# Decoder layer on one core: FFN stages one tile nearer to the attention, z and hidden scales computed apart, the last norms in two steps of the tail

## What is computed

```python
x = x + attn(layernorm(x))      # q * scan(kv, sigmoid(a)): a gated recurrence over the sequence
x = x + xattn(layernorm(x))     # 16 heads over 64 context rows and a null row, Wout, layernorm, scale and bias
x = x + ffn(layernorm(x))

def act_quant(x):               # per row
    scale = 127.0 / clip(max(abs(x), axis=-1), 1e-5)
    return clip(round(x * scale), -128, 127) / scale
def ffn(x):                     # weights are ternary, 256 -> 1024 -> 256
    h = silu(bitlinear(x, w_gate)) * bitlinear(x, w_up)
    return bitlinear(h, w_down) # bitlinear quantises its input with act_quant
```

## Time and profile before

| | |
|---|---|
| median of 3 runs | 542.71 us (541.34 to 543.03) |
| the profiled execution | 541.14 us, of which the span 539.1 us |
| TensorE busy | 483.1 us (90%) |
| VectorE busy | 425.2 us (79%) |
| ScalarE busy | 327.6 us (61%) |
| GpSimd busy | 304.4 us (56%) |

### The profile page before, as it was taken

How to read it: one execution, slowest core, us unless ns; L and a number is a source line. 1 busy time by engine, 2 the same in 40 slices (tenths; PEclk the granted TensorE clock), 3 DMA queues, 4 the chain that set the end, 5 groups by cost and what they waited for, 6 DMA issues and landing times.

```text
span 539.1 us, 9354 instructions
## 1 busy us (share of the span) xinstructions
PE 483.1 (90%) x2974; PEld 390.8 (72%) x3002; DVE 425.2 (79%) x937; ACT 327.6 (61%) x452; POOL 304.4 (56%) x482
## 2 busy tenths in 40 slices
PE   1889999999988988999999999999999999997662
PEld 1666787777767888877877887878778878776321
DVE  5899998958527666888888888888888888875863
ACT  4422233356333443797888877878888778866450
POOL 2211323710001567778787877787878777888631
PEclk9999999999999999999999999999999999999995
DMA  8992000000000000011322121212111322122342
GB/s 284 364 400 85 1 0 1 0 2 1 1 0 1 1 2 5 7 30 35 47 44 49 36 55 35 50 36 55 40 45 36 47 47 45 36 54 50 69 97 68
DMA packets 57949, 30.49 MB, mean 57 GB/s; under 512 B 44336, under 2 KB 55856, under 8 KB 57904
## 3 DMA queue, kind: packets, MB, share of 16 engines
q1 hardware_dynamic: 57904, 29.93, 21.5%
HBM read 15.24 MB, written 4.19 MB: 36 GB/s over the span
## 4 chain that ended last, share of the span: by engine, by line
POOL 32%; issue 23%; PE 20%; DVE 18%; DMA 4%; ACT 2%; POOLq 1%; DVEq 1%; ACTq 0%
PE psum L1130 9%; POOL region_d L529 5%; POOL region_d L507 3%; POOL xs L509 3%; POOL region_d L505 3%; PE psum L1146 3%; POOL sc L539 3%; POOL sc L552 3%; DVE region_a L871 3%; POOL region_d L563 2%; POOL region_d L520 2%; POOL region_c L568 2%; PE psum L1387 2%; DMA region_d<-region_d 2%; PE psum L1392 2%
## 5 line engine op out<-in xcount | busy, mean ns | idle before, releaser
L517 POOL TENSOR_TENSOR region_d<-region_d,rden 128x1024 f32<-128x1024 f32 x32 | 60.9, 1902 | 103.4 <-DVE rden L998 103.4
L1130 PE MATMUL psum<-Mhi,xT2hi 128*128 128x260 f32 x256 | 75.0, 293 | 0.2
L1130 PE MATMUL psum<-Mhi,xT2lo 128*128 128x260 f32 x256 | 72.4, 283 | 0.0
L1130 PE MATMUL psum<-Mlo,xT2hi 128*128 128x260 f32 x256 | 72.4, 283 | 0.0
L1387 PE MATMUL psum<-VW,region_d 128*128 128x256 f32 x256 | 61.1, 381 | 4.6 <-DVE pTn L1047 4.6
L1392 PE MATMUL psum<-VW,region_d 128*128 128x256 f32 x256 | 60.5, 379 | 0.0
L1011 DVE SCALAR_TENSOR_TENSOR region_c<-psum,zw,region_c 128x1024 f32<-128x1024 f32 x29 | 37.2, 1283 | 28.7 <-ACT region_c L689 28.6
L1387 PEld LDWEIGHTS psum<-VW,region_d 128*128 128x128 f32 x256 | 48.1, 190 | 14.6 <-DVE pTn L1047 6.0
L1392 PEld LDWEIGHTS psum<-VW,region_d 128*128 128x128 f32 x256 | 48.6, 190 | 6.6
L677 ACT ACTIVATE region_d<-psum,sc 128x256 f32<-128x256 f32 x32 | 18.0, 564 | 53.9 <-POOL sc L556 53.1
L981 DVE TENSOR_REDUCE mx<-psum 128x8 f32<-128x520 f32 x64 | 44.2, 691 | 6.6 <-PE psum L1130 5.3
(11 more groups left out here) (150 smaller groups left out, 1253.5 us busy)
## 6 DMA issues: line engine op xcount, KB each, us to landing
out_dram<-xs SPq DMA_DIRECT2D x32, 128.0 KB, 1.9
xs<-in_x_dram SPq DMA_DIRECT2D x1, 2560.0 KB, 16.5
VW<-in_L_xattn_Wkv_dram SPq DMA_DIRECT2D x1, 2048.0 KB, 17.3
region_b<-in_L_xattn_Wkv_dram SPq DMA_DIRECT2D x1, 2048.0 KB, 17.6
xs<-in_x_dram SPq DMA_DIRECT2D x3, 512.0 KB, 6.5
region_w<-in_L_ffn_w_gate_dram SPq DMA_DIRECT2D x1, 1024.0 KB, 10.1
region_w<-in_L_ffn_w_up_dram SPq DMA_DIRECT2D x1, 1024.0 KB, 12.5
region_w<-in_L_ffn_w_down_dram SPq DMA_DIRECT2D x1, 1024.0 KB, 16.6
```

What stands on the lines that cost most here:

```text
L517: pool.tensor_tensor(p2[:, v, 0:H * MK].rearrange("p (h j) -> p h j", j=MK), e[:, :, 0:MK], rden[:, v, :].unsqueeze(2).broadcast_to([P, H, ...
L1130: mm = pe.matmul(dst, lhsT, rhs, start=i == 0, stop=i == len(terms) - 1)
```

## The change

The FFN stages of a tile move one step nearer to its attention: gate, up, silu and hidden row are those of tile n - 4 in step n, quantisation, cast and transpose of the hidden row those of n - 5, down, residual and store those of n - 6. The loop has one step less (to T + 5). `norm3` stays with tile n - 3, but stands on ScalarE right behind `norm_out` in all steps; the maximum and scale of z stand on VectorE ahead of `exp_sum`; the quantisation of z stands on GpSimd between the output and the probabilities. The scale of the hidden row has instructions of its own in all steps. The waits for `consts_set` that stood beside other waits in this loop are gone. In the tail, the norms of the tiles 29 to 31 are done in the steps 32 and 33.

```diff
-            for n in range(-2, T + 7):
+            for n in range(-2, T + 6):
...
             def stages2_3(n, u4):
-                u, v = u4 % 2, 1 - u4 % 2
+                if n == T:
+                    deviation4(T - 2)
+                    quantise_z(T - 3)
+                if n == T + 1:
+                    quantise_z(T - 1)
                 if exists(n - 1, T):
...
+                    add_output(n - 1)
+                if not late(n) and exists(n - 3, T):
+                    quantise_z(n - 3)
                 if exists(n + 1, T):
...
+                    probabilities(n + 1)
+                if exists(n - 5, T):
+                    cast_h(n - 5)
+                if n == T:
+                    deviation4(T - 1)
+                    quantise_z(T - 2)
+                if not late(n) and exists(n - 2, T):
+                    deviation4(n - 2)
                 if exists(n, T):
...
+                    deviation3(n)
             steps(stages2_3)
...
-                    count, = registers(pool, n + 1)
-                    pool.wait_ge(consts_set, 2)
-                    pool.wait_ge(rstd3_done, count)
...
-                if late(n) and exists(n - 3, T):
-                    norm3(n, v)
+                if n <= T and exists(n - 3, T):
+                    norm3(n - 3)
+                if n == T + 1:
+                    norm3(T - 1)
                 if exists(n, T):
...
+                if late(n) and exists(n - 4, T):
+                    silu_gate(n - 4, False)
+                if exists(n - 5, T):
+                    quantise_h(n - 5, n)
+                if n == T:
+                    norm3(T - 2)
+                if not late(n) and exists(n - 4, T):
+                    silu_gate(n - 4, n < T - 1)
                 if even:
...
+            def scale_hidden(t, v):
+
+                dve.wait_ge(hmax_done, t + 1)
+                dve.tensor_scalar(qs[:, v, 0:1], amax[:, v, 0:1], CLIP, 1.0 / QMAX, ALU.max, ALU.mult) \
+                    .then_inc(qsh_done, 1)
+                dve.wait_ge(qsh_done, t + 1)
+                dve.reciprocal(qr[:, v, 0:1], qs[:, v, 0:1]).then_inc(qrh_done, 1)
+                hidden_weight(t, v)
...
+                if exists(n - 3, T) and n <= T:
+                    z_max(n - 3)
+                    scale_z(n - 3)
                 if not head and exists(n + 1, T):
                     exp_sum(n + 1, v)
...
+                if not late(n) and exists(n - 4, T):
+                    hidden_layer(n - 4, n)
+                if n == T + 1:
+                    z_max(T - 1)
+                    scale_z(T - 1)
...
                 if late(n):
-                    residual(n - 7)
...
+                    residual(n - 6)
+                    if exists(n - 4, T):
+                        hidden_layer(n - 4, n)
+                if exists(n - 4, T):
+                    hidden_max(n - 4, v)
+                    scale_hidden(n - 4, v)
+                if n == T:
+                    stats4(T - 1)
+                    mean4(T - 1)
+                    z_max(T - 2)
+                    scale_z(T - 2)
+                if not late(n) and exists(n - 6, T):
+                    residual(n - 6)
```

More of the change, by code:

```diff
@@ L377, in late, with hidden @@
             return isinstance(n, int) and n >= T
-        def hidden(n):
-            return h3[1 if isinstance(n, int) and n >= T - 5 and (n - (T - 5)) % 2 == 0 else 0]
+        def hidden(t):
+            return h3[1 if t >= T - 4 and (t - (T - 4)) % 2 == 0 else 0]
         def half(n):
@@ new lines, in cast_h, with deviation4 @@
+            def cast_h(t):
+                pool.wait_ge(hq_done, t + 1)
+                if t > 0:
+                    pool.wait_ge(nhT_ready[(t - 1) % 2], 16 * ((t - 1) // 2 + 1))
+                pool.tensor_copy(nh3, nq3).then_inc(nh_ready, 1)
+            def deviation4(t):
+                u = t % 2
+                pool.wait_ge(mv4_done, t + 1)
+                if t > 1:
+                    pool.wait_ge(z_ready, t - 1)
+                pool.tensor_scalar(sc4[:, u, 0:1], mv4[:, u, 1:2], 1e-5, None, ALU.add).then_inc(ve4_done, 1)
+                pool.wait_ge(ve4_done, t + 1)
+                pool.tensor_tensor(sc4[:, u, 1:2], sc4[:, u, 0:1], expo[:, 0:1], ALU.pow).then_inc(rstd4_done, 1)
+                pool.wait_ge(rstd4_done, t + 1)
+                pool.tensor_scalar(sc4[:, u, 2:3], mv4[:, u, 0:1], sc4[:, u, 1:2], -1.0, ALU.mult, ALU.mult) \
+                    .then_inc(nmr4_done, 1)
@@ new lines, in quantise_z @@
+            def quantise_z(t):
+                v = t % 2
+                pool.wait_ge(qr_done, t + 1)
+                pool.tensor_scalar(z3[:, v, :], z3[:, v, :], qr[:, v, 1:2], MAGIC, ALU.mult, ALU.add) \
+                    .then_inc(zq_done, 1)
+                pool.wait_ge(zq_done, t + 1)
+                if t > 1:
+                    pool.wait_ge(nT_ready[v], 16 * (t // 2))
+                pool.tensor_scalar(n3[:, v, :], z3[:, v, :], 1.0, -MAGIC, ALU.mult, ALU.add).then_inc(n3_ready, 1)
@@ L739, in stages2_3 @@
                         .then_inc(pT1_ready, 1)
-                if late(n) and exists(n - 5, T):
-                    silu_gate(n, v)
-                if exists(n - 6, T):
-                    if n - 1 < T:
-                        act.wait_ge(qr_done, n - 3)
-                    else:
-                        act.wait_ge(qrh_done, n - T)
-                    if positive(n - 6):
-                        act.wait_ge(nh_ready, n - 6)
-                    act.activation(nq3, hidden(n - 6), ACT.Copy, scale=qr[:, u, 0:1]).then_inc(hq_done, 1)
-                if not late(n) and exists(n - 5, T):
-                    silu_gate(n, v)
-                if not late(n) and exists(n - 3, T):
-                    norm3(n, v)
+                if late(n) and exists(n - 4, T):
+                    silu_gate(n - 4, False)
+                if exists(n - 5, T):
+                    quantise_h(n - 5, n)
[3 more added lines that the diff above has]
+                    silu_gate(n - 4, n < T - 1)
                 if even:
@@ L1063, in stages2_3 @@
                 if not head and exists(n + 1, T):
                     exp_sum_reciprocal(n + 1, v)
[L1065 to L1077 removed]
+                if exists(n - 2, T) and n <= T:
+                    mean4(n - 2)
@@ L1119, in stages2_3 @@
-                if exists(n - 7, T) and not late(n):
-                    residual(n - 7)
+                if late(n):
+                    residual(n - 6)
[4 more added lines that the diff above has]
+                    scale_hidden(n - 4, v)
+                if n == T:
+                    stats4(T - 1)
+                    mean4(T - 1)
+                    z_max(T - 2)
+                    scale_z(T - 2)
@@ L1379, in stages2_3 @@
                     scores_half(n + 2, 1, (u4 + 2) % 4, half(n + 2 - u), batch(n + 2))
-                if exists(n + 2, T) and exists(n - 5, T):
-                    gate_up(n, v)
+                if exists(n + 2, T) and exists(n - 4, T):
+                    gate_up(n - 4, n)
                 if exists(n, T):
```

291 lines of the change are left out of this document (126 added, 165 removed).

## The result

The changed kernel takes 554.34 us (median of 4 runs, 553.52 to 557.02) against 542.87 us for the kernel before beside it (541.34 to 543.17): ratio 1.020, 95% interval 1.016 to 1.024: slower, clear of noise, though not surely by 2%. The profiled execution took 553.68 us, its span is 551.8. Renumbered lines: `norm_out` L677 is now L706, norm3 L697 is L733, the first copy L733 is L771, L736 is L774, the silu L689 is L718, the hidden row L1011 is L1042, L1047 is L1115, `exp_sum` L993 is L1024, the probabilities L517 are L529, and L556 is L565.

The account below looks back on a forecast made before the run. A two-step ring of ScalarE, VectorE and GpSimd was taken as the bound; 4.6 + 4.8 + 1.15 - 1.5 = +9.05 us on 541.14 (profiled) or 542.71 (median) gives 550.2 or 551.8; forecast 551.0, range 544.5 to 555.5.

Parts of the forecast that it names:

- the ring of two steps: Chain through ScalarE, VectorE and GpSimd whose legs fill the 21.46 us of two steps; forecast +0.5, to 21.96.
- faster: Rival: the ring does not close, idle time is true slack, norm3 and z block cost nothing; 537 us; chance 0.10.
- nearly cancel: Rival: removed waits give 0.4, the extra pair costs nothing, the tail gives back 3; 541 to 544 us; chance 0.10.
- slower still: Rival: late z quantisation holds the probabilities, 558 us, or queued SP transposes hold down in the tail, 1.5 us; chance 0.10.
- the drain: Rival: a drain behind each table load in the one more FFN step, 553 us; chance 0.02.
- The sum of two steps: Period of two steady steps: 21.46 + 0.50 (norm3) + 0.20 (scale pair) - 0.20 (waits for constants) = 21.96 us.
- Extra scale pair: On VectorE's leg, separate scale instructions for z and hidden row: +0.20 us net in two steps, bounds nothing and 0.45.
- Waits for the constants: On GpSimd's leg, removing waits for `consts_set` shortens two steps by 0.2 us, bounds 0 and 0.4.
- nothing in the steady steps: TensorE's order of work stays the same, so it was to add no time to the steady steps.
- The stretches: Forecast by `norm_out` starts: steps 3 to 10 +4.6, 10 to 30 +4.8, 30 and 31 +1.15, tail -1.5 us.
- The second ring: Chain without silu, `norm_out` through copies, z block, `exp_sum` and GpSimd: 10.57 us, odd steps 0.61 more, two steps at least 21.75.
- the tail's terms: Cast 27 some 7.2 us behind tile 31's `norm_out`, cast chain 19.76 and last 8.7 us unchanged; one step less gives -1.5.

Follow-up runs that it names:

- place_only: Kernel before, distances kept, with norm3, z block and z quantisation at the changed places and separate scale pairs; waits for constants stay: 557.28 us, ratio 1.023.
- norm3_first: Changed kernel with norm3 ahead of `norm_out` in the steps before the tail: 547.47 us, ratio 1.006.
- split_scales: Kernel before with one scale pair for z and one for the hidden row, at the same place in the step: 544.20 us, ratio 1.001.
- no_consts: Kernel before without the waits for the constants in the loop: 541.42 us, ratio 0.996.
- z_first: norm3_first with VectorE's z block ahead of the low part L1115: 554.67 us, ratio 1.019.
- z_first_two: z_first with the 128x2 product of z's weights written as two of 128x1: 548.95 us, ratio 1.011.
- tail_order: Changed kernel with hidden-row casts 27 and 28 moved earlier in the two refilled tail steps, SP transposing the hidden row first: 555.44 us, ratio 1.022.
- early_z_two: early_z with the 128x2 product of z's weights written as two of 128x1: 534.99 us, ratio 0.985.
- early_z: Kernel before, its distances and tail, with norm3 ahead of `norm_out`, z block ahead of the hidden row, scales apart, no loop waits for constants: 546.45 us, ratio 1.005.
- early_z_late_zw: early_z with the 128x2 product of z's weights put behind the hidden row: 541.93 us, ratio 0.997.
- shift_only: Changed kernel's nearer FFN distances with the old places of norm3, z block, z quantisation and the SP transposes: 593.36 us, ratio 1.093.
- before_two: Kernel before with the 128x2 product of z's weights written as two of 128x1 at its old place: 544.81 us, ratio 1.004.

## Why the prediction was right, and where it was off

The forecast was 551.0 us, slower with 0.84, range 544.5 to 555.5; the median is 554.34.

*The mechanism* held: the ring of two steps, norm3 on it, `norm_out` waiting in every step. Of the marks given ahead: norm3 starts 0.46 us behind `norm_out` (0.47 foreseen), the next copy 0.49 behind that (0.50), the z block takes 0.83 (0.82), the gap ahead of L565 is 0.10 (0.08), cast 27 comes 7.06 us behind `norm_out` (7.2), the end 35.6 behind it (over 35). place_only and norm3_first show the places as the cause, and norm3 as 0.44 us of two steps. The rivals "faster" and "nearly cancel" fall; so does the first half of "slower still", since the quantisation of z ends 0.76 us before the probabilities start (its second half, two transposes queued in the tail, was not looked into); the drain does too: the silu still starts 1.30 us behind the start of its table load (369.12 to 370.42), which in the Trainium skill, "ScalarE: Activation LUTs", What ACT_TABLE_LOAD costs, would take about 2.66.

*The sum of two steps* came out 0.12 short, 21.96 for 22.08, and three of its terms were mis-sized, by the legs above:
- Extra scale pair: +0.20 foreseen; split_scales +0.09. On VectorE's leg the z block comes in at 0.83 where 0.75 go out (361.64 to the residual at 365.75 is 4.11 us in the trace of before, and 371.73 to 375.09, 3.36, after).
- Waits for the constants: -0.20 foreseen; GpSimd's leg shrinks by 0.12, and no_consts gained 0.05 in two steps.
- Missed: +0.20 on VectorE's leg, where the halves of the scores' maxima start later. I had TensorE's part as "nothing in the steady steps". But with norm3 on the ring, the input norm L683 ends later against TensorE's program, the transposes L1310 wait for it 10 times from 250 to 480 us (7.5 us; in the trace of before once, 0.4), and the scores end 0.04 us ahead of the second maximum that reads them (376.98 and 377.02). VectorE's 0.2 us is read off the rows, and norm3_first, where that wait is 0.3 instead of 0.8, has it too. In both kernels each maximum starts 0.03 to 0.04 us behind the end of the scores that it reads, in the trace of before 0.21 and 0.11; what exactly sets it was not isolated.

*The stretches:* steps 3 to 10 +4.6 foreseen, +5.3 measured (step 3 10.43 for 10.4, step 4 9.66 for 9.6, steps 5 to 9 55.4 for 54.9); 10 to 30 +4.8 and +6.1 (ten pairs at 0.62); 30 to 32 +1.15 and +1.0; the tail -1.5 and -1.54. That is +10.9 for +9.05. The rest of the difference between the two spans, 1.8, lies ahead of step 3, with the lower clock: 5 us at 0.66 are 1.7 us of TensorE's time at full clock (an estimate from that row). It was in no term of the sum.

*The second ring*, without the silu, was put at 10.57 in even steps; it is 10.64, and sets these steps. But z_first and z_first_two, which shortened exactly this one (to 10.29), gained nothing: the ring over two steps took it back in the odd ones. That the even steps' wait is an opening was my error in the experiments, not in the prediction.

*What the tail's terms say:* one step less gave back 1.5 us, as worked out, and the casts' chain has the same 19.75 us. That the start of cast 27 sets the end, as my sum has it, is borne out only in part: in tail_order it came 3.9 us earlier and the end did not, since the chain hangs on the z of the last tiles as well. The number is right; some of it may be luck.

## What to carry to other kernels

When an instruction is moved, ask which leg of the ring it lands on, and add it over the whole period: a step in which an engine still waits gives nothing back if the ring spans two. Put it in the wait that the ring itself makes (norm3 ahead of `norm_out`, the z block ahead of the hidden row), not behind the work that ends this wait; here, at the same distances, place_only cost 2.3% and early_z_two gained 1.5%. (The two also differ in the place of the quantisation of z, the waits for the constants and the form of the product; without the new form early_z lost 0.5%.) And look at the duration of a moved instruction at its new place, not only at its old one: what runs on GpSimd beside it can make 0.2 us into 1.3.

## What the runs showed of the hardware

- VectorE's multiplication of 128x2 with all operands in SBUF did not finish while a wide GpSimd instruction (128x80 to 128x1024) that had started before it was running: beside GpSimd's probabilities it took 1.33 us (early_z), beside an addition 0.45 to 0.72 (z_first), beside the cast 0.83 (early_z_late_zw), each time ending 0.01 to 0.04 us behind GpSimd's instruction; alone 0.21. Scales, reciprocals and products of 128x1 took 0.15 to 0.21 beside the same ones. The Trainium skill, "SBUF — State Buffer", Who interferes with whom, says that GpSimd shares a port pair with VectorE, that a VectorE instruction in a two-port mode and a GpSimd instruction lock it for their whole duration, and that the later one blocks fully: by that, the traces agree for the wide instructions. Beside a GpSimd instruction of 128x1 that had started before it, the 128x2 product took its 0.21 us all the same (shift_only: 534.24 to 534.45, GpSimd's 533.97 to 534.54), which that rule does not foresee. What no run here shows is which mode the 128x2 form was in.
- The profiles differ in two places by 1.6 to 2.0 us each, whatever the edit: the start of step 3 (200.1 to 200.3, or 201.9 to 202.2 with the dip of the granted clock; norm3_first alone has 201.0, without a dip), and the last cast to the end (8.7 to 8.8, or 10.6 us, the latter in early_z, early_z_two and before_two). There is one profile of each kernel, so that executions of one kernel differ in the same places is a guess; two such places would make up at most 4 of the 5.5 us between the times of the kernel before (541.0 to 546.5). What sets them was not tried.
